# Row-tiled masks in a cross-attention kernel, with other places for mask loads, weight loads and one projection

## The reference, cut to what matters

```python
q = split(layernorm(x) @ Wq.T + bq); k = split(ctx @ Wk.T + bk); v = split(ctx @ Wv.T + bv)
scores = einsum('bhqd,bhkd->bhqk', q, k) / sqrt(8)
scores = where(mask[:, None, :, :], finfo.min, scores)
merged = einsum('bhqk,bhkd->bhqd', softmax(scores), v)      # heads side by side
x = x + tanh(g_xattn) * (merged @ Wo.T + bo)
n = layernorm(x)
w = normalised(max(softmax(n @ Wg + bg) - sigmoid(n @ Wt + bt) * 0.125, 0))
x = x + tanh(g_ffn) * sum_e w[e] * (gelu(n @ W1[e] + b1[e]) @ W2[e] + b2[e])
```

## Time and profile before

| | |
|---|---|
| time, median of 3 runs | 627.77 us (626.75 to 628.27) |
| the profiled execution | 625.05 us, its span 623.2 us |
| PE, PEld busy | 593.8 us (95%), 452.0 us (73%) |
| DVE, ACT, POOL busy | 479.4 us (77%), 378.6 us (61%), 178.9 us (29%) |
| mean granted clock of TensorE | 0.981 |

### The profile page before, as it was taken

One profiled execution on the slowest core, in us unless ns is written; L12 is line 12 of the kernel. 1 busy time (PEld: TensorE's weight loads), 2 busy tenths in 40 slices (PEclk: granted clock), 3 DMA queues, 4 the chain that ended last, 5 costly groups with the idle time before them and its releaser, 6 DMA issues.

```text
span 623.2 us, 13765 instructions
## 1 busy us (share of the span) xinstructions
PE 593.8 (95%) x4490; PEld 452.0 (73%) x4490; DVE 479.4 (77%) x940; ACT 378.6 (61%) x625; POOL 178.9 (29%) x224
## 2 busy tenths in 40 slices
PE   7699899999999998999999999999999999999998
PEld 6556566666666655788878788787887887887886
DVE  3457677777776776578879788888888888888886
ACT  2134455555555545767777677677677676776673
POOL 7523344444444221212113212212112112121121
PEclk9969899999999999999999999999999999999999
DMA  6854556555655520041121121111121121111210
GB/s 183 223 150 129 153 160 175 142 141 151 172 150 152 160 64 5 3 102 44 44 68 35 56 68 52 50 57 44 50 67 50 34 67 50 50 61 40 67 51 17
DMA packets 43998, 55.12 MB, mean 88 GB/s; under 512 B 9520, under 2 KB 27824, under 8 KB 42416
## 3 DMA queue, kind: packets, MB, share of 16 engines
q1 hardware_dynamic: 43504, 53.99, 30.5%
q10 hardware_dynamic: 448, 0.53, 0.2%
HBM read 39.16 MB, written 14.81 MB: 87 GB/s over the span
## 4 chain that ended last, share of the span: by engine, by line
PE 82%; DMA 6%; ACT 4%; SPq 4%; DVE 2%; issue 2%; ACTq 0%; DVEq 0%
PE ps_h L1059 10%; PE ps_h L1061 9%; PE ps_h L1060 9%; PE ps_y L1074 9%; PE ps_y L1076 9%; PE ps_y L1075 9%; PE misc L1037 4%; DMA kq_st<-maxT 4%; PE scores L975 4%; PE scores L1003 3%; PE scores L1015 3%; PE scores L992 2%; ACT probs L559 2%; PE misc L1114 1%; DMA kq_scratch<-kq_parts 1%
## 5 line engine op out<-in xcount | busy, mean ns | idle before, releaser
L583 ACT ACTIVATE h_sb<-ps_h,b_sb 128x512 f32<-128x512 f32 x256 | 176.1, 690 | 102.1 <-PE ps_h L1061 92.1
L742 DVE TENSOR_TENSOR h_low<-h_sb,h_high 128x512 fp32r<-128x512 f32 x256 | 164.5, 682 | 0.1
L522 POOL TENSOR_TENSOR yT<-yT,weighted 128x512 f32<-128x512 f32 x54 | 70.9, 1313 | 277.9 <-DVE weighted L917 277.9
L738 DVE CAST h_high<-h_sb 128x512 fp32r<-128x512 f32 x128 | 97.7, 763 | 52.9 <-ACT h_sb L583 52.7
L719 DVE TENSOR_REDUCE neg_max<-scores 128x8 f32<-128x1024 f32 x64 | 77.9, 1221 | 49.1 <-PE scores L975 49.1
L1059 PE MATMUL ps_h<-x_high,w_high 128*128 (+1 forms) x256 | 101.9, 398 | 2.1 <-ACT h_sb L583 2.0
L1074 PE MATMUL ps_y<-h_high,w_high 128*128 128x512 f32 x256 | 100.2, 391 | 0.3 <-ACT h_high L587 0.3
L1061 PE MATMUL ps_h<-x_high,w_low 128*128 (+1 forms) x256 | 99.8, 390 | 0.0
L1076 PE MATMUL ps_y<-h_high,w_low 128*128 128x512 f32 x256 | 99.7, 389 | 0.0
L1060 PE MATMUL ps_h<-x_low,w_high 128*128 (+1 forms) x256 | 99.7, 389 | 0.0
L1075 PE MATMUL ps_y<-h_low,w_high 128*128 128x512 f32 x256 | 99.6, 389 | 0.0
(11 more groups left out here) (127 smaller groups left out, 720.9 us busy)
## 6 DMA issues: line engine op xcount, KB each, us to landing
w_row<-w_scratch SPq DMA_DIRECT2D x64, 256.0 KB, 3.1
kq_st<-kq_scratch SPq DMA_DIRECT2D x64, 192.0 KB
kq_scratch<-kq_parts SPq DMA_DIRECT2D x30, 256.0 KB, 3.2
w_raw<-in_w_ffn SPq DMA_DIRECT2D x16, 256.0 KB, 3.7
kq_scratch<-kq_parts SPq DMA_DIRECT2D x32, 128.0 KB, 3.3
ctx_sb<-in_ctx SPq DMA_DIRECT2D x16, 128.0 KB, 2.6
out_y<-y_out SPq DMA_DIRECT2D x7, 256.0 KB, 2.3
x_all<-in_x SPq DMA_DIRECT2D x13, 128.0 KB, 2.2
```

Of the source, the lines that this page charges most:

```text
L583: nc.scalar.activation(h_sb[:, j % HBUF, :], ps_h[:, j % 4, :], ACT.Gelu_apprx_tanh, bias=b1_sb[:, j:j + 1]).then_inc(h_done, 1)
L738: nc.vector.tensor_copy(h_high[:, j % HBUF, :], h_sb[:, j % HBUF, :]).then_inc(high_odd, 1)
L742: nc.vector.tensor_tensor(h_low[:, j % HBUF, :], h_sb[:, j % HBUF, :], h_high[:, j % HBUF, :].bitcast(F32), ALU.subtract).then_inc(low2_do ...
```

## The change

It has four parts.

1. Masks. The mask of a batch was one tile of 128 queries by 128 keys, and a mask matmul used all 128 rows of the array: natural 4 a batch, 512 columns each; transposed 4 a batch, 512 columns each. Now every row group of 32 partitions holds the whole mask, 4 queries to a partition (`mask_b` has an index j of 4), and a mask matmul uses 32 rows: natural 16 a batch on 32x32 tiles with 512 columns; transposed 16 a batch on 32x128 tiles with 128 columns. Queries are therefore dealt out (query 4i + j stands at place 32j + i): the transposes of `xn` write with a stride, and the copies to `headsT` put the order back. The mask's DMA goes four times over 32 KB a group, in 512 B pieces instead of 128 B, as two transfers; the cast on GpSimd has 1024 elements a partition instead of 256. `mask_words`, `merged`, `mergedT` and `x2n` have one buffer instead of two.
2. SP's turn. Masks and contexts stay ahead of the stacks; expert weights and x are issued after max0, ahead of the stores. The six small weight loads of `later_weights` go to the end of step 0, from ahead of max0.
3. PE's turn. The transposed scores of batch 0 stand ahead of the projection v. On VectorE `inT_low` stands ahead of `v_pad`. ScalarE's turn is as before.
4. Start. Three more idle matmuls ahead of the first transposed scores, and six instead of two ahead of the first max0.

```diff
-        mask_words = sa("mask_words", [P, 2, GB, S // 4], I32)
-        mask_b = sa("mask_b", [P, 2, GB, S], BF16)
+        mask_words = sa("mask_words", [P, GB, S], I32)
+        mask_b = sa("mask_b", [P, 2, GB, 4, S], BF16)
...
+            def load_mask(g):
+                for b in range(GB):
+                    every = bass.AP(a["mask"].tensor, (g * GB + b) * 32 * S, [[0, ROWS], [S, 32], [1, S]])
+                    sp.dma_start(mask_words[:, b, :], every).then_inc(mask_in[g % 2], 16)
...
                 if it != -1:
-                    inputs_ahead(it)
+                    masks_and_contexts(it)
                 stacks(it)
...
+                if it != -1:
+                    weights_and_x(it)
                 stores(it)
                 if it == -1:
-                    inputs_ahead(it)
+                    masks_and_contexts(it)
+                    weights_and_x(it)
+                elif it == 0:
+                    later_weights()
...
-                    nc.gpsimd.tensor_copy(mask_b[:, u, :, :], mask_words[:, u, :, :].bitcast(U8)).then_inc(mask_done, 1)
+                    nc.gpsimd.tensor_copy(mask_b[:, u, :, :, :].rearrange("p b j k -> p b (j k)"), mask_words[:].bitcast(U8)).then_inc(mask_done, 1)
...
-                    nc.scalar.activation(headsT[:, 0, :], misc[:, bank_of("V0"), 0:2 * P], ACT.Copy)
+                    nc.scalar.activation(headsT[:, 0, :].rearrange("p (k i j) -> p k j i", k=2, j=4),
+                                         misc[:, bank_of("V0"), 0:2 * P].rearrange("p (k j i) -> p k j i", k=2, j=4), ACT.Copy)
...
-            def natural_mask(r, b, u):
-                return mm(scores[:, r, :].rearrange("p (s k) -> p s k", s=SLABS), masked_ident[:],
-                          mask_b[:, u, b, :].unsqueeze(1).to_broadcast([P, SLABS, S]), start=False, stop=True)
+            def natural_mask(pair, b, u):
+                for j in range(4):
+                    for r in pair:
+                        rows = slice(32 * r, 32 * r + 32)
+                        ins = mm(scores[32 * j:32 * j + 32, r, :].rearrange("p (s k) -> p s k", s=SLABS), masked_ident[rows, rows],
+                                 mask_b[rows, u, b, j, :].unsqueeze(1).to_broadcast([32, SLABS, S]), start=False, stop=True)
+                return ins
...
-            def transposed_mask(r, b, u):
-                return mm(scores[:, 2 + r, :].rearrange("p (s q) -> p s q", s=SLABS), mask_b[:, u, b, :],
-                          masked_ident[:].unsqueeze(1).to_broadcast([P, SLABS, S]), start=False, stop=True)
+            def transposed_mask(pair, b, u):
+                for j in range(4):
+                    for r in pair:
+                        rows = slice(32 * r, 32 * r + 32)
+                        ins = mm(scores[:, 2 + r, :].rearrange("p (s j i) -> p j s i", s=SLABS, j=4)[:, j], mask_b[rows, u, b, j, :],
+                                 masked_ident[rows, rows].unsqueeze(1).to_broadcast([32, SLABS, 32]), start=False, stop=(j == 3))
+                return ins
```

More of the change, by code:

```diff
@@ L154, in gated_block @@
         rstd2 = sa("rstd2", [P, 2, GB], F32)
-        x2n = sa("x2n", [P, 2, GB, D], F32)
+        x2n = sa("x2n", [P, GB, D], F32)
         x2T = sa("x2T_sb", [P, 2, GT], F32)
@@ L352, in rows_of, with masks_and_contexts @@
                 return kq_dram[g].rearrange("(r c d) (s x) -> c (d s) r x", r=ROWS, c=3, s=SLABS)[c]
[L354 to L360, removed]
+            def masks_and_contexts(it):
+                if (g := group_at(it, 1)) is not None:
+                    if g > 0:
+                        sp.wait_ge(mask_done, g)
+                        load_mask(g)
                 if (g := group_at(it, 4)) is not None:
@@ L841, in body @@
                     max_split(g, 1)
+                if (g := group_at(it, 3)) is not None:
+                    u = g % 2
+                    dve.wait_ge(high_done, g + 1)
+                    nc.vector.tensor_tensor(inT_low[:, u, :], misc[:, bank_of("inputs"), :], inT_high[:, u, :].bitcast(F32),
+                                            ALU.subtract).then_inc(misc_read[bank_of("inputs")], 1)
+                    if g == 0:
+                        statistics(1)
                 if (g := group_at(it, 1)) is not None:
@@ L1092, in body @@
                     misc_wait_read(pe, "heads", g)
-                    turn("merged", g, lambda b: merged[:, u, b * H:(b + 1) * H, :].rearrange("p h d -> p (h d)"))
+                    turn("merged", g, lambda b: merged[:, b * H:(b + 1) * H, :].rearrange("p h d -> p (h d)"))
                 if (g := group_at(it, -3)) is not None:
@@ L1098, in body @@
                         pe.wait_ge(g_copied, 1)
-                    turn("x2T", g, lambda b: x2n[:, u, b, :])
+                    turn("x2T", g, lambda b: x2n[:, b, :])
                     if g == NG - 1:
@@ L1170, in body @@
                     natural_rest(g, 1, u)
+                if (g := group_at(it, 0)) is not None:
+                    u = g % 2
+                    transposed(g, 0, u)
+                    transposed_rest(g, 0, u)
                 if (g := group_at(it, 1)) is not None:
@@ L1184, in body @@
                     ins.then_inc(misc_full[bank_of("v")], 1)
-                if (g := group_at(it, 0)) is not None:
-                    u = g % 2
-                    transposed(g, 0, u)
-                    transposed_rest(g, 0, u)
                 if (g := group_at(it, -4)) is not None:
```

85 lines of the change are left out of this document (40 added, 45 removed).

## The result

The changed kernel takes 684.88 us (median of 4 runs, 682.33 to 687.62), the kernel before 627.26 us beside it; the ratio is 1.0946, with an interval of 1.0848 to 1.1043. Forecast were 632.3 us and a range of 621 to 641: the direction was right, the size was not: +57.6 us against +4.5. The profiled execution took 682.63 us, its span is 680.6 us and the mean granted clock 0.88.

What follows compares the result with a forecast made beforehand. Two closed loops through DMA, not PE's busy time, were taken to bound phase A. Start -4.3, eight steps +9.4, last three +0.15 and last masks -0.8 made +4.5 on 627.77: 632.3 us, range 621 to 641.

Steps and rivals of the forecast that it cites:

- What bounds the kernel now: Phase A steps of 13.77 us: two closed loops from T, the start of batch 0's transposed scores, to the next T.
- PE's busy time decides neither: Phase A: PE, busy for 150.70 of 159 us, looks like the bound, but the two loops were taken to decide.
- The first loop: From T (batch 0's transposed scores start) through max1, SP's issue, the stacks and max0's landing to next T; 13.88 us.
- The loops after: Middle steps: first loop 5.15 + 2.75 + 7.0 + 0.05 = 14.95 us, second 14.1; +1.18 a step.
- slower still: Rival: natural mask tiles of one row group run serially, or the clock falls to 0.5 in waits; 643 us, chance 0.15.
- The start: Group 0's T at 32.4 us, -1.85; first four steps 57.4 instead of 59.9, -2.5; together -4.3.
- PE is not their bound after: First four steps, slow at 0.86 of the clock: PE would not bound them after the change; 57.4 us forecast.
- PE's turn: First loop: v behind T delays inT_high, VectorE and max1; T to max1's issue 5.15 us instead of 2.94, +2.2.
- Masks: Mask matmuls on PE: about -0.45 us a transposed batch; -0.2 a natural pair, four times a group.
- the third rival: The rival "slower still": natural mask tiles run one behind the other, deciding from a pair of 0.6 us; chance 0.15.
- covered: Mask DMA of 96 KB more and longer GpSimd cast: no cost if the mask is ready 13 us later.
- SP's turn and start: Max1's issue to the stacks' 2.75 us instead of 3.29; stacks' issue to T 7.0 instead of 7.65; group 0's T 32.4.

Runs made afterwards that it cites:

- e1: SP's new turn alone, on the kernel before: masks and contexts ahead of the stacks, expert weights and x behind max0; 619.74 us, ratio 0.9913.
- g1: SP's new turn with the start's seven more idle matmuls, on the kernel before; 618.70 us, ratio 0.9897.
- w3: The changed kernel with the old masks, and 14 unused full-array matmuls of 256 columns behind v in each step; 643.26 us, ratio 1.0291.
- w1: The changed kernel with the old masks; SP's turn, start and turns of PE and VectorE stay as changed; 656.01 us, ratio 1.0501.
- d1: The row-tiled masks alone, on the kernel before, with the old turns and start; 669.91 us, ratio 1.0718.
- b1: The turns of PE and VectorE alone, on the kernel before, with full-width masks and SP's old turn; 662.14 us, ratio 1.0583.
- w2: The changed kernel with the old masks and VectorE's turn as before (v_pad ahead of inT_low); 643.18 us, ratio 1.0260.
- n1: The kernel before with three quarters of each mask matmul's columns left out, 128 instead of 512, over the full array; 630.93 us, ratio 1.0101.
- u1: The row-tiled masks alone, with mask loads of 8 KB instead of 64 KB from group 2 on; 656.24 us, no ratio.
- a1: The changed kernel with the turns of PE and VectorE put back; 665.9 us (654.59 to 669.81), no ratio.
- k1: The row-tiled masks alone, with two full-width matmuls of zeros ahead of each pair of masks; 681.12 us, ratio 1.0898.
- h1: The changed kernel with VectorE's order as before, v_pad ahead of inT_low; 676.64 us, ratio 1.0833.
- u2: The changed kernel with mask loads of 8 KB instead of 64 KB from group 2 on; 687.03 us, no ratio.

## Why the prediction was wrong

**"What bounds the kernel now", and "PE's busy time decides neither".** This is the step that failed. The first loop was read rightly, but TensorE's own list was a third limit, and it was as long: 13.23 busy and 0.54 idle in a step of 13.77. e1 shows it. SP's turn takes the three parts of the loop from 13.58 to 12.85, and the step stays at 13.76:

```profile
90.82:200.88 110.06, 106.75 (x1425) 71.67 (x1425) 83.84 (x221) 60.48 (x112) 49.71 (x77) 1.00 0.56 155
```

In the kernel before, T starts at most 0.5 us behind max0's landing, in four of the eight steps 0.04. In e1 it starts 0.7 to 1.6 us behind it in every step: the DMA is in time, TensorE is not. A TensorE at 95% was not free to take a pause of 2 us in each step.

**"The loops after": 14.95 at full clock.** A middle step of the changed kernel takes 17.25. Of the 2.30 that were missing, 0.33 lie between T and max1's issue (5.48 for 5.15), 0.2 from there to the stacks (2.98 for 2.75), and 1.8 behind the stacks' issue: 8.46 to max0's landing and 0.33 more to T, for a forecast of 7.0. So the loop alone, measured, makes 16.9 of the 17.25, and the term that was mis-sized most is the stacks' time. But it is not the only limit, as the kernels with light loads or old masks show: there T comes late for the DMA, by TensorE's own list. For that list the sum took every row at a clock of 1.00. w3 is this loop without the clock's fall and without the masks, and its step is 15.44; the same with the clock falling, w1, is 16.61. The time fell into the rivals' "slower still" (637 and more, 0.15), not by its first mechanism, serial tiles. The falling clock did stand there, as good for 643 us; that is a quarter of the loss that came, as it was not worked out what half a clock does to TensorE's own list.

**"The start" and the last steps.** The four steps after T of group 0 were forecast at 57.4, since "PE is not their bound after". With the old masks and SP's turn they take 58.00 (e1) and, at full clock, 55.52 (g1): near it. In the changed kernel they take 72.83, and the clock is at 0.5 without a break from 39.2 to 87.0 us. The last three take 54.51 for 39.45, at 0.63. These seven steps hold 30 of the 53 us. The table of the stretches shows parts of it (d1, w1); how the whole divides between clock, loads and pause stays open.

**PE's turn: +2.2 between T and max1.** Right: 5.35 in the step shown against 5.15, on the mean 5.49, and 3.14 before. The working even had `v_pad` at 3.30 behind T; that the gate, which is next on TensorE, waits for it was not drawn from it. The turns of PE and VectorE alone cost 36 us (b1), with SP's turn and the start as changed 37 (w1 against g1). VectorE's part of this is 13 us (w2).

**Masks: -0.45 a transposed batch, -0.2 a natural pair.** The transposed ones take 0.37 up to v where the old took 0.88: right. A natural pair takes 0.34 to the next instruction at full clock, for a forecast of 0.22; the old pair took 0.52 in the median and 0.44 at the least, so it saves 0.1 to 0.18 of the 0.2 that were said, and the eight tiles do not run one after another (the third rival; 0.6 was its threshold). The strided copies to `headsT` take 0.62 us for 0.38, within the bound that was given, and the cast on GpSimd 1.04, as estimated. But the 1.2 us a step saved on TensorE bought no time. Less work in a step of the same length is more idle time, and the clock fell with it: n1 shows this on the kernel before, with only columns left out.

**Loads of the masks: "covered".** Wrong, and this is what the stacks' 7.0 us had not counted. They are covered as the mask's own arrival goes; but they stand ahead of the stacks, which land 8.65 us after their issue instead of 7.30 (d1), and 6.92 with light loads (u1). In the changed kernel it is 8.05.

**SP's turn and start.** Right where the masks are the old ones: 2.33 for a forecast of 2.75, 7.24 for 7.0, T of group 0 at 32.83 (e1) for 32.4. With the new masks, the stacks of group 1 are issued at 25.78 us and land 9.4 us later, where e1 issues them at 24.41 and has them 7.6 us later; T is at 35.64.

**How the 57 us are made.** The masks alone cost 45, the turns alone 36, and SP's turn gains 6 (with the start 6 too). The sum would be 75, and 57 came. The masks cost 29 on top of the rest (changed against w1), the turns 30 (changed against a1's 654.59; 19 by its median). The costs overlap. That a half clock and a late DMA are paid only once, whichever part brings them, would explain it, but was not tested. Shown are: the clock that falls in w1 stays up when the pause is filled (w3), fewer columns lower it (n1), more raise it (k1), and the loads delay the stacks (d1, u1). Not settled is why a shorter pause left the clock lower with the new masks (h1, 0.74 for 0.79), whether lighter loads gain anything on the changed kernel (u2), and how its 6.8 us at 0.5 a step divide between pause and masks.

The Trainium skill (TensorE: Matmul & The Clock Gate, section HAM oscillation — how this bites in real kernels) tells of a kernel whose clock falls again at each wait for a DMA, between bursts of work that are shorter than the wait. w1 agrees that it comes back step after step (in seven of eight); it differs in that TensorE is busy there for 14.3 of 16.6 us, and that the single long pause is 2.0 us.

## What to carry to other kernels

Where TensorE is busy above 90%, add its own list to the loops: busy, pauses and the clock. Here a new pause of 2 us in a step cost 2.9 us of it (w1 against g1), and a saving of 1.2 us was worth nothing, so move work ahead of a wait only if something else fills the hole. Before taking work off TensorE in such a kernel, leave some of it out and time that, as n1 does: where the time does not fall, there is nothing to gain yet. And a transfer that is early enough for its reader can still be late for the one behind it in the queue.

## What the runs showed of the hardware

- More work made a kernel faster: 112 matmuls of 256 columns in eight steps, in a pause of 2.0 us (14 in each of the other steps too), took 656.0 to 643.3 us; the granted clock of these steps rose from 0.91 to 1.00.
- Less work made a kernel slower, if by little: masks of 128 instead of 512 columns, 1.0101 of the time (1.0033 to 1.0169), clock of the middle steps 0.86 instead of 1.00.
- A shorter pause did not by itself raise the clock: 0.7 instead of 2.0 us at the gate with row-tiled masks, 0.74 instead of 0.79 (h1, changed).
- Seven idle matmuls more at the start (nine instead of two) keep the clock of g1 at 1.0 from 16.5 us on, where e1 has 17.1 us at 0.5 after that; on the time it is 1 us, less than the runs tell apart.
- Sixteen matmuls on 32x128 tiles with 128 columns take 0.37 us, eight on 32x32 tiles with 512 columns, two row groups with four column groups each, 0.34, both to the next instruction and at full clock.
